# Head groups outside the batch rows, with the router, the shared slices and the expert tiles inside the attention steps

## The chip, the cores and the metric

One core of one Trainium2 chip runs the kernel. The metric is the device time of one execution in microseconds. The profile is of one execution. Names of engines: TensorE (PE in the rows, PEld its weight loads), VectorE (DVE), ScalarE (ACT), GpSimd (POOL) and SyncE (SP), which issues most of the DMAs.

## The reference, cut to what matters

```
x: [4, 512, 512]; xn = layernorm(x); out = x + attention(xn) + experts(xn)
attention, per batch row, 32 heads of 128 in 8 groups of 4 that share k and v, chunks of 128 tokens:
  q, k, v, gate = xn @ Wq.T, Wk.T, Wv.T, Wg.T;  rope on q and k
  dt = softplus(xn @ Win.T + dt_bias);  G = cumsum in the chunk of dt * -exp(A_log_bias)
  y = ((q k^T) * causal exp(G_i - G_j)) (v dt) + exp(G) q @ state;  state = exp(G_last) state + k_dec^T (v dt)
  y = y / rms(y) * gnorm_w * silu(gate);  sum over the heads of y @ Wo.T
experts, per token: 16 experts in 4 groups, best 2 groups by the router, best 2 experts in them;
  silu(x w1 + b1) * (x w2 + b2) @ w3 + b3, weighted, plus a shared one of 2 slices of 128
```

## The kernel before, in words

All products are made from high and low parts: each fp32 operand is copied to fp32r by ScalarE (the high part), the low part is the difference, made by POOL or VectorE, and `mm3` (L1083) issues three matmuls, high by high, high by low and low by high.

The kernel begins with a prologue that loads x, normalises 16 tiles of 128 tokens, turns them, computes the decay coefficients and the router's logits. The normalised and turned rows of the first half (two of the four batch rows) stay in SBUF as `xnh` and `xnl`; those of the second half go to memory. `end_phase` (L409) is where all engines meet before the first step.

Then `attention(half)` runs twice. In it a loop over the 8 head groups `kv` holds two steps, b = 0 and 1, one for each batch row of the half. So there are 32 steps in all, 16 in each half. `acc` holds the sums of 8 tiles in SBUF, and the weights of every head group are loaded and split in each half again. A step, on TensorE: projections of k, v and four heads of q, with transposes of v and k; the first out-projection (`out_proj`, L1125) of the step before, which lags one step; then the first gate projection, `scores(0)` (L1166), and a loop over the four chunks with the chunk's state (`chunk_state`), `inter`, a gate projection, `intra` (L1197), the next `scores`, `squares` and further out-projections. On VectorE: five ropes (`rope`, L1519), the low part of the values (`vw_lo`), of the fourth q (`q3lo`, L1582) and of k; then in the chunk loop `late_z` (L1497), `wlo`, `late_acc` (L1504), the state, its low part (L1621), `weigh` (L1543) and `gated` (L1565). ScalarE makes the high parts (`rope_hi`, `z_hi`, `vw_hi`, `split_hi` L811), the exponentials, the tanh of the gate (`silu_gate`, L921) and the rms batch (`rms_batch`, L858: two table loads, a Ln and an Exp over 2048 columns). POOL makes low parts (`split_lo` L643, `rope_lo`, `z_lo` L422) and the masked decay exponents (`gmasked`).

The order of each engine is written out by hand and kept by semaphores; an engine never passes over an instruction that waits. Weights come as pieces of 256 KB through two buffers, `stage`: SyncE issues piece n (`piece`, L439) when POOL has split piece n - 2, ScalarE then makes the high part and POOL the low part. `gload` (L489) brings the decay exponents of a chunk, broadcast to all partitions. On SyncE `hold` (L404) is a wait.

Between the halves stand the shared slices of the first half (`shared_up` L1288, `shared_down` L1308, `h_mul` L1654), the routing (`route_scores` L1682 to `route_slots` L1711) and the exchange of `acc` and xn. After the second half come the shared slices of that half and 48 expert tiles of 128 gathered tokens each: `turn_x` (L1340), `expert_up` (L1349), `turn_h` (L1362), `expert_down` (L1368). Their weights come in two DMAs per tile (`weights`, L583) into two buffers each; the expert's number is read from a table `etab` by SyncE. Last, the two picked rows of every token are gathered and added to the sums (`add_picked`, L1815).

```
e = sp.value_load(etab[0:1, bass.ds(k, 1)], min_val=0, max_val=E - 1)   # L584
hold(sp, m12_lo, k + 1)
sp.dma_start(raw12[par], row[:, 0:1024]).then_inc(m12_in[par], 16)      # L587
```

## Time and profile before

| | us |
|---|---|
| median of 3 runs (2355.04 to 2359.32) | 2358.24 |
| the profiled execution, its own time | 2350.6 |
| its span, first to last instruction | 2348.8 |

In the page of that execution TensorE is busy for 2134.9 us (91%), VectorE for 1836.9 (78%), ScalarE for 1403.2 (60%) and POOL for 1076.4 (46%), and 198.61 MB move by DMA. A row of a timeline gives the start, the duration, the engine, the line of the kernel, what is written and read, and in brackets the idle time ahead of it with what ended it. "issue" there means that the profile shows nothing that the engine waited for. A matmul's duration reaches from the start of its read to a modelled end, so successive ones overlap; the distance of the starts is its price. A window's row gives what each engine was busy in that stretch. TensorE's clock was granted in full (1.00, 2.4 GHz) or at half (1.2 GHz); the mean over the span is 0.973.

### The profile page before, as it was taken

The page shows a single profiled execution, that of the slowest core. Times are in us where ns is not written, and L with a number is a line of the kernel's source. Part 1 is how long each engine was busy: PE and PEld are TensorE (multiplying, and loading weights), DVE is VectorE, ACT ScalarE, POOL GpSimd, SP SyncE. Part 2 cuts the span into 40 slices and gives each one's busy share as a digit, 9 for nine tenths or more (in the row PEclk, how much of TensorE's full clock was granted, in tenths as well). Part 3 has the DMA queues.
Part 4 walks back from the last instruction along what each step waited for, and adds up shares of the span by engine and source line. Part 5 has one row for each costly group of instructions (what it writes and reads, how often), then busy time and mean ns, then how long its engine had stood idle before and what let it go on. Part 6 is the DMA issues. An engine that isn't in the chain of part 4 may idle for free.

```text
span 2348.8 us, 35057 instructions
## 1 busy us (share of the span) xinstructions
PE 2134.9 (91%) x9788; PEld 1687.2 (72%) x9788; DVE 1836.9 (78%) x3422; ACT 1403.2 (60%) x2716; POOL 1076.4 (46%) x840
## 2 busy tenths in 40 slices
PE   6599999999999999996999999999999999777884
PEld 6477777777777777774777777777777777555653
DVE  3488888888888888865888888888888888466665
ACT  2366666666666666653666666666666666455550
POOL 6245454545354544443454555454545455422216
PEclk9899999999999999997999999999999999898897
DMA  4312121212121212124121212121211121387777
GB/s 171 128 41 64 36 63 36 70 37 63 36 63 36 63 36 66 41 77 157 40 68 36 63 36 63 36 63 37 65 45 54 49 53 50 113 259 247 251 238 237
DMA packets 155566, 198.61 MB, mean 85 GB/s; under 512 B 13831, under 2 KB 90215, under 8 KB 155518
## 3 DMA queue, kind: packets, MB, share of 16 engines
q1 hardware_dynamic: 139742, 163.86, 23.8%
q0 software_dynamic: 7424, 21.00, 3.0%
q10 hardware_dynamic: 8352, 13.17, 1.5%
q8 instruction: 23, 0.38, 0.1%
q14 instruction: 25, 0.20, 0.0%
HBM read 169.65 MB, written 28.33 MB: 84 GB/s over the span
## 4 chain that ended last, share of the span: by engine, by line
issue 41%; POOL 26%; DVE 11%; PE 8%; DMA 7%; ACT 3%; SPq 2%; POOLq 1%; DVEq 0%; ACTq 0%
POOL gm L687 5%; POOL zl L425 5%; DMA gate<-in_wm 4%; POOL ql L694 3%; POOL wol L646 3%; POOL wgl L646 3%; POOL wql L646 2%; POOL vl L708 2%; DVE vwl L1557 1%; DMA gbc<-decay_exponents 1%; POOL kl L694 1%; DVE ql L1789 1%; POOL wkvl L646 1%; ACT qh L1030 1%; DVE yb L1501 1%
## 5 line engine op out<-in xcount | busy, mean ns | idle before, releaser
L425 POOL TENSOR_TENSOR zl<-yb,zh 128x512 fp32r<-128x512 f32 x130 | 172.6, 1328 | 348.5 <-ACT zh L872 348.3
L1085 PE MATMUL OU<-woh,zh 128*128 128x512 f32 x520 | 243.8, 469 | 16.3 <-POOL wol L646 11.9
L1085 PE MATMUL PJ<-xnh,wqh 128*128 128x512 f32 x544 | 225.9, 415 | 24.4 <-DVE t L1538 22.6
L1536 DVE TENSOR_TENSOR t<-PJ,cosb 128x512 f32<-128x512 f32 x160 | 110.2, 689 | 176.0 <-PE PJ L1087 132.8
L1087 PE MATMUL PJ<-xnh,wql 128*128 128x512 f32 x544 | 215.8, 397 | 0.0
L1086 PE MATMUL PJ<-xnl,wqh 128*128 128x512 f32 x544 | 215.3, 396 | 0.0
L890 ACT ACTIVATE qh<-t 128x512 fp32r<-128x512 f32 x128 | 81.0, 633 | 221.5 <-DVE t L1541 221.5
L1085 PE MATMUL PJ<-xnh,wgh 128*128 128x512 f32 x512 | 204.7, 400 | 0.0
L1087 PE MATMUL OU<-woh,zl 128*128 128x512 f32 x520 | 204.5, 393 | 0.0
L1086 PE MATMUL OU<-wol,zh 128*128 128x512 f32 x520 | 204.0, 392 | 0.0
L1087 PE MATMUL PJ<-xnh,wgl 128*128 128x512 f32 x512 | 200.4, 391 | 0.0
L1086 PE MATMUL PJ<-xnl,wgh 128*128 128x512 f32 x512 | 199.5, 390 | 0.0
L687 POOL TENSOR_TENSOR gm<-gbc,amask 128x512 f32<-128x512 f32 x128 | 166.1, 1298 | 49.6 <-DMA gbc<-decay_exponents 27.9
L1557 DVE SCALAR_TENSOR_TENSOR vwl<-vf,hcoef,vwh 128x128 fp32r<-128x128 f32 x384 | 180.3, 527 | 0.0
L646 POOL TENSOR_TENSOR wol<-stage,woh 128x512 fp32r<-128x512 f32 x64 | 88.7, 1406 | 169.7 <-ACT woh L814 169.7
L1541 DVE TENSOR_TENSOR t<-t 128x512 f32<-128x512 f32 x160 | 161.8, 1011 | 5.6
L897 ACT ACTIVATE gm<-gm,hcoef 128x128 f32<-128x128 f32 x512 | 162.1, 388 | 0.0
L646 POOL TENSOR_TENSOR wgl<-stage,wgh 128x512 fp32r<-128x512 f32 (+1 forms) x72 | 96.7, 1362 | 141.4 <-ACT wgh L814 141.4
L694 POOL TENSOR_TENSOR ql<-t,qh 128x512 fp32r<-128x512 f32 x96 | 137.1, 1440 | 41.4 <-ACT qh L890 41.4
L968 ACT ACTIVATE sth<-st 128x512 fp32r<-128x512 f32 x96 | 60.7, 633 | 144.6 <-DVE st L1612 96.5
L1085 PEld LDWEIGHTS PJ<-xnh,wqh 128*128 128x128 f32 x544 | 104.0, 191 | 58.7 <-DVE t L1538 38.4
L1085 PEld LDWEIGHTS OU<-woh,zh 128*128 128x128 f32 x520 | 98.1, 189 | 63.5 <-issue 41.3
(479 smaller groups left out, 6550.9 us busy)
## 6 DMA issues: line engine op xcount, KB each, us to landing
gbc<-decay_exponents SPq DMA_DIRECT2D x128, 256.0 KB, 4.8
gate<-in_wm SPq DMA_DIRECT2D x48, 512.0 KB, 4.5
stage<-in_wq SPq DMA_DIRECT2D x72, 256.0 KB, 3.9
stage<-in_wg SPq DMA_DIRECT2D x64, 256.0 KB, 2.7
stage<-in_wo SPq DMA_DIRECT2D x64, 256.0 KB, 2.7
gbc<-in_wm SPq DMA_DIRECT2D x48, 256.0 KB, 4.1
expert_rows<-rs ACTq DMA_DIRECT2D x48, 256.0 KB, 4.1
stage<-in_wkv SPq DMA_DIRECT2D x34, 256.0 KB, 2.7
```

The costliest lines, as they stand in the source:

```text
L425: nc.gpsimd.tensor_tensor(lo[:], yb[:, c, :], hi[:].bitcast(F32), ALU.subtract).then_inc(S["zlo"], 1)
L646: g.tensor_tensor(lo_out, stage[:, n[1], 0:lo_out.shape[-1]], hi_out.bitcast(F32), ALU.subtract).then_inc(wsplit_lo, 1)
L687: g.tensor_tensor(gm[:, c % 2, :].rearrange("p (h i) -> p h i", h=HG), gbc[:, c % 2, :].rearrange("p (h i) -> p h i", h=HG), amask[:].unsq ...
L694: g.tensor_tensor(lo, t2[:, (5 * b + i) % 2, :], hi.bitcast(F32), ALU.subtract).then_inc(S["ropelo"], 1)
L890: a.activation(hi, t2[:, (5 * b + i) % 2, :], ACT.Copy).then_inc(S["ropehi"], 1)
L897: ins = a.activation(gv, gv, ACT.Exp, bias=head(0, c, h))
L1085: nc.tensor.matmul(out_, a_hi, b_hi, start=first, stop=False)
L1086: nc.tensor.matmul(out_, a_hi, b_lo, start=False, stop=False)
L1087: return nc.tensor.matmul(out_, a_lo, b_hi, start=False, stop=last)
L1536: v.tensor_tensor(t1[:], PJ[bank][:], cosb[:], ALU.mult)
L1541: v.tensor_tensor(t2[:, slot, :], t1[:], t2[:, slot, :], ALU.add).then_inc(S["rope"], 1)
L1557: ins = v.scalar_tensor_tensor(vwl[:, hs], vf[:, c * P:(c + 1) * P], head(2, c, h), vwh[:, hs].bitcast(F32), ALU.mult, ALU.subtract)
```

## The change: what it does

The loop over head groups is outermost: for each of the 8 groups there are four steps, one for each batch row (b = 0 to 3), 32 in all, written out in full instead of two loops of eight turns. Each weight piece is loaded and split once. The turned rows of all four batch rows go to memory in the prologue and come back in every step (`xn_load`: eight loads of 256 KB into a ring of six). The sums of a batch row, `acc`, are 4 tiles; each is stored to memory after its add (`acc_store`) and loaded for another row (`acc_load`, which holds until the store has landed). The coefficients of a step are loaded too, sorted in memory; 16 copies on POOL sort them in the prologue.

The routing is cut into about 20 parts, each behind one rope of VectorE in steps 0 to 4. The scatters of the slot table stand on POOL in steps 5 to 10. In steps 4 to 11 (`SHARED`) TensorE does one batch row's part of a shared slice in chunk 3, and the down product is added to the next step's out-projections. In steps 13 to 28 each step carries three expert tiles u, u + 1 and u + 2 (`m` is true). The weights of a tile come in three pieces A, B and C through the same `stage` buffers; A and B are the up weights, C the down weights, and they share two pairs of SBUF tiles, so that B of tile v takes the place of C of v - 1. ScalarE makes the high and POOL the low parts (VectorE made the low parts before). The gathered rows, their parts and the bias rows have one buffer each. In steps 29 to 31 and at the end `late_acc` also adds the picked rows. At the end one flush of four out-projections remains. The bias of the down product comes as three small matmuls.

The core of the diff (SyncE, then ScalarE, TensorE and VectorE):

```diff
-HALVES = 2
-ROWS = B // HALVES
-NT = ROWS * NCH
-STEPS = KV * ROWS
...
+STEPS = KV * B
+SHARED = range(B, 3 * B)
+SCATTERED = range(5, 11)
+FIRST_EXPERT = 13
+LAST = STEPS - B
...
+    def unit_bias(v):
+        if v == 0:
+            At(sp, FIRST_EXPERT).before("oproj", 4)
+        else:
+            hold(sp, m_dn, v)
+        e = sp.value_load(etab[0:1, v:v + 1], min_val=0, max_val=E - 1)
+        row = bdram[bass.ds(e, 1), :, :].rearrange("o r n -> (o r) n")
+        sp.dma_start(plain(fhh[0:2, P:512]), row[:, 0:384]).then_inc(mb_in, 16)
+        sp.dma_start(plain(fhl[0:2, P:512]), row[:, 384:768]).then_inc(mb_in, 16)
...
+    def acc_store(s, c):
+        kv, b = (s - 1) // B, (s - 1) % B
+        At(sp, s).wait("accd", c + 1)
+        t = b * NCH + c
+        dst = out[t // NT, t % NT] if kv == KV - 1 else accd[t]
+        sp.dma_start(dst, acc[:, c, :]).then_inc(acc_out[c], 16)
+    def acc_load(s, c):
+        kv, b = (s - 1) // B, (s - 1) % B
+        hold(sp, acc_out[c], 16 * (s - 1))
+        t = b * NCH + c
+        sp.dma_start(acc[:, c, :], xv[:, t, :] if kv == 0 else accd[t]).then_inc(acc_in[c], 16)
...
-        with sp.Fori(0, KV) as kv:
-            for b in range(ROWS):
...
+        first_pieces((0, 1))
+        if m:
+            if u == 0:
+                unit_piece("A", 0)
+            unit_piece("B", u)
+            unit_bias(u)
+        gload(0)
+        gload(1)
+        if s >= 2:
+            acc_store(s - 1, 3)
+            acc_load(s, 3)
+        first_pieces((2, 3))
+        if s + 1 < STEPS:
+            hcoef_load(s + 1)
+            if s == 0:
+                hold(sp, x0_out, 32)
+                for j in range(4):
+                    hold(sp, xts_out[j], 96)
+            else:
+                At(sp, s - 1).wait("proj", 10)
+                if s - 1 in SHARED:
+                    hold(sp, u_up, s - B)
+            xn_load(s + 1, (0, 1))
+        gload(2)
+        if m:
+            unit_piece("C", u)
+            unit_piece("A", u + 1)
+        if m:
+            unit_bias(u + 1)
+            unit_piece("B", u + 1)
+            unit_piece("C", u + 1)
+            unit_piece("A", u + 2)
+        if s:
+            acc_store(s, 0)
+            acc_load(s + 1, 0)
+        if b == B - 1 and kv + 1 < KV:
+            for j in range(2):
+                piece(("wkv", kv + 1, j), wkv[kv + 1, j])
+        shared_piece(0)
+        shared_piece(1)
+        gload(3)
+        if m:
+            unit_bias(u + 2)
+            unit_piece("B", u + 2)
+        if s:
+            acc_store(s, 1)
+            acc_load(s + 1, 1)
+        if m:
+            unit_piece("C", u + 2)
+            unit_piece("A", u + 3)
+        if b == B - 1 and kv + 1 < KV:
+            piece(("wq", kv + 1, 0), wq[kv + 1, 0])
+            piece(("wq", kv + 1, 1), wq[kv + 1, 1])
+        if s:
+            acc_store(s, 2)
+        if b == B - 1 and kv + 1 < KV:
+            piece(("wq", kv + 1, 2), wq[kv + 1, 2])
+            piece(("wq", kv + 1, 3), wq[kv + 1, 3])
+        if s:
+            acc_load(s + 1, 2)
+        if s + 1 < STEPS:
+            at.wait("proj", 10)
+            if s in SHARED:
+                hold(sp, u_up, s - B + 1)
+            xn_load(s + 1, (2, 3))
+        shared_piece(2)
...
+        first_piece(1)
+        if m:
+            if u == 0:
+                split_hi(("A", 0))
+            split_hi(("B", u))
+        if s:
+            rms_batch(at)
+        if m:
+            x_hi(u, 0)
+        rope_hi(0, kh[:])
...
+        rope_hi(4, qh[:, 3, :])
+        if m:
+            h_hi(u)
+        if s:
+            z_hi(at, 1)
+        if m:
+            evict(u, 0)
+            x_hi(u + 1, 1)
+            split_hi(("B", u + 1))
+            store(u)
+        silu_gate(0)
+        if m:
+            m_tan(u + 1, 1)
+            split_hi(("C", u + 1))
...
+                at.wait("stt", c + 1)
+                if c:
+                    at.wait("yinter", c)
+                a.activation(sth[:], st[:], ACT.Copy).then_inc(S["sthi"], 1)
+                if m and c == 1:
+                    m_tan(u + 2, 2)
+                    split_hi(("C", u + 2))
+                    split_hi(("A", u + 3))
+                if b == B - 1:
+                    for j in (2 * c, 2 * c + 1):
+                        split_hi(("wkv", kv + 1, j) if j < 2 else ("wq", kv + 1, j - 2))
+                if b == 0 and s in SHARED and c == 0:
+                    split_hi(("ws", kv - 1, 0))
+                    split_hi(("ws", kv - 1, 1))
+                silu_gate(c + 1)
+                if m and c == 0:
+                    h_hi(u + 1)
+                    x_hi(u + 2, 2)
+                if m and c == 1:
+                    h_hi(u + 2)
+                exp_g(c + 1)
+            if c:
...
+        if m:
+            at.before("y", 4)
+            if u:
+                pe.wait_ge(m_h, u)
+            expert_up(u, 0)
+        for j in (2, 3):
+            at.wait("roperd", j)
+            proj_q(j)
+        if m:
+            turn_h(u)
+        if s:
+            if b == 1:
+                need(("wo", kv, 3))
+            out_proj(at, 0)
+        if m:
+            at.before("wsc", 4)
+            expert_down(u, 0)
+            turn_x(u + 1, 1)
+        if b == 0:
+            need(("wg", kv, 3))
+        at.wait("roperd", 4)
+        proj_g(0)
+        if m:
+            expert_up(u + 1, 1)
+        at.wait("ropelo", 4)
+        at.wait("q3lo", 1)
+        if m:
+            pe.wait_ge(m_ev, u + 1)
+        scores(0)
...
+            if m and c == 1:
+                expert_up(u + 2, 2)
+            if m and c == 3:
+                at.wait("stt", 3)
+                expert_down(u + 2, 2)
+            if s in SHARED and c == 3:
+                at.wait("stt", 3)
+                at.wait("gated", 3)
+                shared_up(s - B)
+            if s == RANKED and c == 3:
+                at.wait("stt", 3)
+                pe.wait_ge(rk_made, 1)
+                mflat = msum.rearrange("p t n -> p (t n)")
+                nc.tensor.matmul(CS[:, 0:256], upper[:], mflat, start=True, stop=True)
+                nc.tensor.matmul(CS[:, 256:512], ones[:], mflat, start=True, stop=True).then_inc(rk_done, 1)
+            if c < 3:
+                if c == 0:
+                    at.wait("roperd", 5)
+                else:
+                    at.wait("gated", c)
+                proj_g(c + 1)
+            if m and c == 0:
+                turn_h(u + 1)
+                turn_x(u + 2, 2)
+            if m and c == 1:
+                at.wait("yt", 1)
+                turn_h(u + 2)
+            intra(c)
+            if c < 3:
+                scores(c + 1)
+            if m and c == 0:
+                at.wait("stt", 1)
+                expert_down(u + 1, 1)
+            if c:
...
+        rope(0, 0)
+        if m:
+            x_low(u, 0)
+        rope(1, 0)
+        if s:
+            late_z(at, 0)
+        rope(2, 1)
+        if m:
+            h_of(u, 0)
+        rope(3, 0)
+        rope(4, 1)
+        if m:
+            h_low(u)
+        dve.wait_ge(hc_in[s % 2], 16 * (s // 2 + 1))
+        vw_lo(0)
+        at.wait("ropehi", 5)
+        v.tensor_tensor(ql[:, 3, :], t2[:, (5 * s + 4) % 2, :], qh[:, 3, :].bitcast(F32),
+                        ALU.subtract).then_inc(S["q3lo"], 1)
+        at.wait("knhi", 1)
+        v.tensor_tensor(knl[:], TR[:, 0:3 * P].rearrange("p (a b) -> p a b", a=3),
+                        knh[:].bitcast(F32), ALU.subtract).then_inc(S["knlo"], 1)
+        if s:
+            late_z(at, 1)
+        if m:
+            x_low(u + 1, 1)
+            gated(0)
+            h_of(u + 1, 1)
+        weigh(0)
...
+            if m and c == 0:
+                h_low(u + 1)
+                x_low(u + 2, 2)
+            if m and c == 1:
+                h_of(u + 2, 2)
+            at.wait("yintra", c + 1)
+            if c:
+                at.wait("yt", c)
+                v.tensor_tensor(yb[:, c, :], YI[:], yb[:, c, :], ALU.add).then_inc(S["y"], 1)
```

## Rows read from the trace of the kernel before

**Rows 1.** Windows by stage: length, busy us of each engine, PEclk, DMA share, GB/s
```profile
98.30:165.90 67.60, 54.13 (x242) 42.83 (x240) 48.81 (x90) 35.28 (x69) 24.42 (x18) 0.90 0.22 60
165.90:1015.10 849.20, 824.69 (x3783) 654.94 (x3781) 729.22 (x1366) 560.57 (x1098) 402.86 (x303) 1.00 0.19 51
1015.10:1071.90 56.80, 52.03 (x206) 38.57 (x204) 36.16 (x76) 19.15 (x26) 19.17 (x14) 0.97 0.36 105
1071.90:1154.30 82.40, 60.16 (x254) 47.75 (x253) 57.26 (x107) 37.61 (x73) 33.19 (x27) 0.83 0.30 96
...
2003.10:2042.00 38.90, 25.43 (x106) 19.87 (x105) 12.75 (x17) 18.57 (x24) 19.09 (x16) 0.87 0.33 106
2042.00:2285.00 243.00, 199.50 (x1040) 149.11 (x1040) 152.08 (x283) 141.77 (x280) 51.68 (x42) 0.91 0.78 247
```
**Rows 2.** Waits of TensorE over the span: us in total, times, longest
```profile
PE SC L1366 <- DVE gm L1804: 43.0, 36, 3.2
PE SC L1085 <- issue: 32.5, 32, 1.6
```
**Rows 3.** Timeline of one step, 392.35 to 448.90: start, us, engine, line, what
```profile
392.35 0.80 PE L1085 MATMUL PJ<-xnh,wkvh 128*128 128x512 f32 x1
...
411.30 0.47 PE L1085 MATMUL OU<-woh,zh 128*128 128x512 f32 x1 [0.74 <-POOL wol L646]
...
414.14 0.39 PE L1085 MATMUL PJ<-xnh,wgh 128*128 128x512 f32 x1
...
414.93 0.90 DVE L1541 TENSOR_TENSOR t<-t 128x512 f32<-128x512 f32 x1
...
416.80 0.68 DVE L1582 TENSOR_TENSOR ql<-t,qh 128x512 fp32r<-128x512 f32 x1
...
417.58 0.47 PE L1085 MATMUL SC<-qh,kh 128*128 128x512 f32 x1 [0.56 <-issue]
...
422.88 0.39 PE L1087 MATMUL SC<-qh,kl 128*128 128x512 f32 x1
...
424.75 0.62 ACT L814 ACTIVATE wkvh<-stage 128x512 fp32r<-128x512 f32 x1
...
424.87 0.69 DVE L1621 TENSOR_TENSOR stl<-st,sth 128x512 fp32r<-128x512 f32 x1 [0.70 <-ACT sth L968]
```
**Rows 4.** Timeline of TensorE over one expert tile
```profile
2185.60 0.59 PE L1085 MATMUL OU<-woh,vwh 128*128 128x512 f32 x1
...
2187.10 0.36 PE L1085 MATMUL TR<-qh,wkvh 128*128 128x256 f32 x1
...
2189.01 0.66 PE L1345 MATMUL PJ<-ident,vf 128*128 128x128 f32 x4
2189.42 0.48 PE L1085 MATMUL YE<-woh,vwh 128*128 128x512 f32 x1
```
**Rows 5.** Window of ScalarE's rms batch: length, busy us, PEclk, DMA share, GB/s
```profile
1021.73:1028.26 6.53, 6.49 (x4) 1.00 0.25 68
```
**Rows 6.** DMA issues by line: KB each, median us from issue to landing
```profile
stage<-in_wkv SPq DMA_DIRECT2D x16, 256.0 KB, 2.7
...
xnl<-turned SPq DMA_DIRECT2D x4, 256.0 KB, 5.1
...
out<-acc SPq DMA_DIRECT2D x8, 256.0 KB, 3.8
```
**Rows 7.** Timeline of SyncE's issues within one tile's loads
```profile
2101.96 0.29 SPq L592 DMA_DIRECT2D zh<-bias_rows  x1
...
2103.84 0.37 SPq L587 DMA_DIRECT2D gate<-in_wm  x1
```
**Rows 8.** POOL's low half of a weight piece, 150 to 1055: ns min/median/max
```profile
L646 POOL TENSOR_TENSOR wol<-stage,woh x32: 1271/1295/1762, 167.7 to 975.9; 128x512 fp32r<-128x512 f32 x32
```
**Rows 9.** Three windows of VectorE's router work between the halves, and their sum
```profile
sum 28.09, DVE 26.14; mean DVE 8.71
```
**Rows 10.** VectorE's add at the end of a rope: ns min/median/max
```profile
L1541 DVE TENSOR_TENSOR t<-t x160: 691/888/1779, 112.7 to 1969.2; 128x512 f32<-128x512 f32 x160
```

1934 lines of the change are left out of this document (861 added, 1073 removed).

## The prediction, made before the changed kernel was run

> **What bounds the kernel now.** The windows by stage come first [rows 1]. In the long attention stretch (15 steps in 849.2 us, so 56.6 us a step; the second half has the same) TensorE is busy for 97% of the time. The other time lies elsewhere: 98.3 us ahead of the first step, 67.6 us in that step, 56.8 us between the halves, 82.4 us in the first step of the second half, and 2348.8 - 2003.1 = 345.7 us at the end, 243 of it in the expert tiles. TensorE's own waits [rows 2] are few: inside attention mostly the one in front of the scores (32.5 us, 32 times), in the expert tiles 43 us on VectorE. Inside a step [rows 3] matmuls of 512 columns start every 0.227 us (13 of them, and the wait of 0.5, lie between 414.14 and 417.58). VectorE ends its low part of q (L1582, at 416.80 + 0.68) 0.1 us before the scores start at 417.58: the wait "issue" is a wait for VectorE. So TensorE sets the pace with VectorE just behind it, 48.6 us busy in the 56.6, and what is put into VectorE's row before the scores delays TensorE.
>
> **What the change removes.** The stage between the halves (56.8), the surplus of the second half's first step (82.4 - 56.6 = 25.8), and the whole end (345.7) go. Step 0 begins on TensorE at 98.3 but ends at 165.9; it now does no out-projection (48 matmuls x 0.227 = 10.9 us) and no rms batch. The exchange of phases stays: 16 small copies on POOL sort the coefficients where a memset of 1.8 us stood, about even. VectorE's 5.7 us of late work also go, so I let it end at 157, which is 8.9 less. Together 437.2; 2348.8 - 437.2 = 1911.6.
>
> **What comes back on TensorE.** Shared slices: 24 matmuls up and 12 down per step, 36 x 0.227 = 8.2, eight times = 65.4; the bias 16 x 0.227 = 3.6. An expert tile [rows 4]: up from 2187.10 to 2189.01 = 1.91, turning the rows to 2189.42 = 0.41, down and turning h 1.50 from 2185.60 to 2187.10, and 0.05 more since three small bias matmuls replace one: 3.87. Times 48 = 185.8. A tail now stands alone after step 31, which in the kernel before lies beside the shared slices: the sum of squares 1.2, table loads, Ln and Exp 6.5 (the whole of [rows 5]), z and its halves 2.9, four out-projections 10.9, the add 0.7, the store 3.8 to 4.3 [rows 6]: 26.6. So with every new wait at nothing: 1911.6 + 65.4 + 3.6 + 185.8 + 26.6 = 2193.0. That is the floor, 6.6% below now.
>
> **The waits that it adds.** One step with tiles (13 to 28) carries three. I walk it from its start, with durations from rows; "T" is the end of the first `expert_down`.
> 1. `h_low` of tile u stands behind the fifth rope on VectorE. In the step shown [rows 3] that rope ends 23.5 us after the start (414.93 + 0.90 against 392.35). `x_low` now waits for ScalarE's table work (+1.5) and `h_of` for its tanh (+1.7, of which 1.0 takes the place of a wait for ql): 25.7, then two ScalarE copies and `h_low`, 1.6: 27.3. TensorE ended its first out-projection at 21.8 (414.14), 0.74 of it waiting for wol; with `turn_x`, up and `turn_h` (2.4) and without that wait and a small one on ropes, it is there at 23.3. Wait 4.0.
> 2. Piece B of tile u+1. SyncE holds until T (`unit_bias` waits for `m_dn`), reads the tile's expert from the table (0.9), then does what lies between 2101.96 and 2103.84 in [rows 7]: two bias rows, a second reading, a hold, the issue. With 0.15 for its hold: T + 2.95. Landing 2.7 [rows 6], ScalarE's half 0.6, POOL's 1.3 [rows 8], hand-overs 0.25: T + 7.8. TensorE has only `turn_x` and one gate projection to do, 3.1. Wait 4.7. ScalarE stands in front of the same piece, and behind it wait the tanh of the gate, `gated` and the weighing of the scores.
> 3. `expert_down` of u+1 stands ahead of the out-projection and needs `h_low`, which stands behind the state's low part. In the step shown the scores end at 423.1 and that low part at 425.5 [rows 3]. With `h_low`: wait 2.6.
> 4. Piece B of u+2: again 7.8 from the second `expert_down`, against 2.7 + 0.7 + 1.4 = 4.8 of work. Wait 3.0, and the next `wfh` waits on ScalarE behind it.
> 5. `turn_h` of u+2 waits for that chain, 1.5.
> Sum 15.8; the wait before the scores and its neighbour, 1.5 to 1.6 a step now [rows 2], lie inside it: 14.3 net, x16 = 229. Bounds for this term: nothing, if SyncE and the queues run ahead of what I read; and 20 a step, if landings take the 3.8 to 5.1 us of the slower rows of [rows 6] and POOL's and ScalarE's queues slip as well.
>
> Smaller ones. **Router**: 26.1 us of VectorE, in three stretches now [rows 9], go into the ropes of steps 1 to 4, 6 to 8 a step. The idle time behind ropes 0 and 3 takes 3 of that: 17 remains. **xn loads**: in the shared steps four 256 KB loads are issued only when `shared_up` is done, 3.8 us before the step ends, and need about 6 (four issues, then 3.5 to 5.1 to landing [rows 6]): 2.2 x 8 = 18, and 2 elsewhere. In other steps they go out behind a store that must land; this just fits. **Steps with b = 3**: the pieces of wkv and wq stand on SyncE behind `acc_store`, and `acc_load` holds until that store has landed (3.8). ScalarE took the first at 424.75 in the step shown [rows 3], and would get it at 428.8; VectorE's 1.5 us of lead takes part. I take 5 us x 7 = 35 (between 0 and 10). The shared pieces likewise, 4 in all. **Picked rows**: two more VectorE adds per chunk (0.7 each) in steps 29 to 31: 13. The step's other loads and stores (2 MB of sums, 2 MB of xn) raise traffic from 51 to some 140 GB/s; the expert stage moves 247 [rows 1], so the bytes themselves cost nothing if the queue's order doesn't.
>
> Sum: 2193.0 + 229 + 17 + 20 + 35 + 4 + 13 = 2511 on the span of 2348.8. The profiled execution took 2350.6 and the median is 2358.2, 9.4 above the span: **2520**.
>
> **A rule against the change.** In this trace VectorE's add of two SBUF tiles (L1541) takes from 0.69 to 1.78 us, median 0.89 [rows 10], with the same operands each time, so what differs runs beside it. The change puts nine more POOL halves, 12 us, into each step with tiles. The Trainium skill, GPSIMD Engine Reference, Key points, says that GpSimd shares its SBUF interfaces with VectorE and contends with instructions that have two SBUF inputs. The median counted above leaves this out; it is the third rival.
>
> **Rivals.**
> A, faster: TensorE finds other work and the tiles cost what they do now, 243 / 48 = 5.06 us each, with the b = 3 terms gone: 2520 - 229 - 35 + 57 = **2313**. For it: the stage of now hides its weight loads with two buffers. Against it: one buffer of each kind, and SyncE's hold at T. It decides once the net wait in a tile step is under 4.2 us (14.3 - 162 / 16). Chance 0.25.
> B, SyncE's row: every `acc_load` waits for a landing, so gloads and xn are late in every step, 4 us x 31 less the 20 counted: **2625**. Against: a store lands in 3.8 [rows 6], and between two of them the step has 8 us or more; the loads are wanted a step later. Chance 0.12.
> C, VectorE beside POOL: of 12 us a quarter meets a two-input instruction (some 12 of its 48.6 us) and holds it up, 3 us x 16: **2568**. Chance 0.12.
> D, the unrolled steps feed TensorE too slowly. The unrolled tile stage shows 199.5 busy and 43 of named waits in its 243 us, so nothing is left for it. At 1 us a step: 2552. Chance 0.03.
>
> **The numbers.** My forecast has 0.48. A gives 0.22 faster and 0.03 within 0.2%, which is about what a measurement of this kernel can tell from no change; all others are slower: 0.24, 0.03, 0.73 with a little of the forecast's lower tail in the first. The forecast's own range is 2420 to 2615 (tile steps at 8 to 20 net); to hold 8 in 10 the whole reaches to 2300, which takes in A.
>
> **What would show it.** Steps without tiles at 57 to 59 us, shared ones at 67, tile steps at 80 to 85. In the list of TensorE's waits: the first matmul of `expert_up` on POOL's low half of a weight piece, 4 to 5 and 3 us, 16 times each; `expert_down` on VectorE's `mhl`. SyncE's holds on PE before the bias rows. A tail of 25 us. The forecast is wrong if tile steps stay under 72 us, or if steps without tiles are above 62.

## The result, and the profile after

The changed kernel takes 2656.1 us (median of 4 runs, 2650.8 to 2664.0) against 2356.9 of the kernel before in the same comparison: ratio 1.127, 95% interval 1.124 to 1.130. Slower, as forecast, but by 299 us where 162 were forecast, and 41 us above the upper end of the range. The profiled execution has a span of 2653.9 us, so 143 us more than the 2511 of the sum.

The windows by stage of the changed kernel, with the columns of [rows 1]: before step 0; step 0; steps 1 to 3; the shared steps 4 to 11; step 12; the 16 tile steps 13 to 28; steps 29 and 30; step 31 with the tail.

```profile
0.00:96.17 96.17, 58.80 (x265) 55.18 (x265) 38.73 (x74) 23.03 (x38) 43.17 (x38) 1.00 0.60 202
96.17:163.36 67.19, 50.16 (x204) 38.20 (x205) 45.34 (x86) 28.09 (x64) 20.77 (x29) 0.87 0.33 99
163.36:361.49 198.13, 179.79 (x775) 137.20 (x773) 169.28 (x320) 107.25 (x208) 64.23 (x49) 0.97 0.29 91
361.49:915.89 554.40, 517.63 (x2298) 403.93 (x2297) 431.39 (x751) 303.50 (x587) 227.23 (x178) 0.99 0.29 92
915.89:974.50 58.61, 57.67 (x264) 45.80 (x265) 51.35 (x93) 35.68 (x70) 24.60 (x18) 1.00 0.35 113
974.50:2433.06 1458.56, 1190.79 (x5186) 923.64 (x5185) 911.06 (x1633) 722.57 (x1448) 571.51 (x456) 0.91 0.36 112
2433.06:2564.07 131.01, 117.26 (x507) 89.46 (x505) 117.51 (x195) 69.76 (x136) 57.45 (x47) 0.96 0.39 117
2564.07:2653.90 89.83, 71.39 (x302) 56.02 (x300) 73.66 (x118) 43.48 (x75) 39.17 (x33) 0.91 0.31 94
```

Set against the sum, stretch by stretch: the end of step 0 is 6 us late (163.4 against 157), steps 1 to 12 take 811 us where 802 were summed, steps 29 to 31 with the tail 221 where it was 209. The tile steps take 1458.6, 91.2 each, where 83.9 were summed: 116 of the 143 us are there. TensorE is busy 82% of that stretch, 1190.8 us, and waits 267.8; its clock was granted at 0.91.

TensorE's waits over the span, for [rows 2]:

```profile
PE SC L1137 <- issue: 103.4, 31, 5.7
PE CS L1137 <- issue: 55.2, 16, 7.4
PE YE L1222 <- DVE upper L1673: 41.7, 23, 2.3
PE YI L1137 <- issue: 40.0, 17, 3.0
PE TR L1339 <- ACT vh L1031: 28.1, 10, 3.2
```

L1137 stands in the helper that issues the three products. The rows are mostly, in order, the waits ahead of `expert_down(u)`, `expert_down(u+1)`, `turn_h`, `expert_up(u+1)` and of K's transposes for V.

Three tile steps in a row, of batch rows 1, 2 and 3 (the same columns as above):

```profile
1339.21:1431.57 92.36, 74.49 (x326) 57.84 (x325) 58.24 (x103) 45.54 (x91) 36.39 (x29) 0.91 0.35 109
1431.57:1516.23 84.66, 71.45 (x326) 55.70 (x325) 56.01 (x103) 43.14 (x87) 31.23 (x25) 0.94 0.36 111
1516.23:1609.81 93.58, 75.52 (x327) 57.99 (x325) 55.98 (x103) 46.69 (x93) 38.89 (x31) 0.89 0.37 118
```

This pattern repeats through all 16: row 2 takes 84.7 to 86.0 us, rows 0 and 1 take 91.5 to 94.3, row 3 takes 93.2 to 95.0. All of them hold three tiles. TensorE's timeline in the middle one, only the instructions that it waited for:

```profile
1458.43 0.77 PE L1137 MATMUL SC<-fbh,fhh 128*128 128x512 f32 x1 [3.73 <-issue]
1468.37 0.36 PE L1137 MATMUL YI<-fah,fch 128*128 128x256 f32 x1 [2.83 <-issue]
1479.09 0.47 PE L1137 MATMUL CS<-fah,fhh 128*128 128x512 f32 x1 [2.46 <-issue]
1488.14 0.35 PE L1137 MATMUL TR<-fbh,fch 128*128 128x256 f32 x1 [1.11 <-issue]
1495.33 0.30 PE L1222 MATMUL YE<-ident,upper 128*128 128x128 f32 x1 [2.26 <-DVE upper L1673]
```

These are the five waits of the prediction, in its order: `expert_down(u)`, `expert_up(u+1)`, `expert_down(u+1)`, `expert_up(u+2)`, `turn_h(u+2)`. It had 4.0, 4.7, 2.6, 3.0 and 1.5, 15.8 in all; here they are 12.4. The waits were found, and in this kind of step they are shorter than forecast, so the surplus must come from elsewhere.

Step 17, of row 1, shows two sources. Its timeline on VectorE, GpSimd, ScalarE and TensorE:

```profile
1357.62 1.29 POOL L789 TENSOR_TENSOR ql<-t,qh 128x512 fp32r<-128x512 f32 x1
...
1358.87 1.29 POOL L467 TENSOR_TENSOR zl<-yb,zh 128x512 fp32r<-128x512 f32 x1
1359.46 3.76 DVE L1711 TENSOR_TENSOR t<-t 128x512 f32<-128x512 f32 x1
...
1360.12 2.55 POOL L711 TENSOR_TENSOR wol<-stage,woh 128x512 fp32r<-128x512 f32 x2
1363.25 0.63 ACT L982 ACTIVATE qh<-t 128x512 fp32r<-128x512 f32 x1 [2.58 <-DVE t L1711]
...
1373.49 0.77 PE L1137 MATMUL SC<-fah,fhh 128*128 128x512 f32 x1 [5.68 <-issue]
...
1377.21 0.63 PE L1138 MATMUL PJ<-xnl,wgh 128*128 128x512 f32 x1
1377.64 0.63 PE L1139 MATMUL PJ<-xnh,wgl 128*128 128x512 f32 x1
```

The addition of two SBUF tiles that ends a rope, 0.69 us at its shortest in [rows 10], takes 3.76 us. GpSimd works without a gap from 1357.62 to 1362.67, four operations of 1.3 us, and the addition ends 0.55 us behind the last. The 16 tile steps have eight such additions of 3.7 to 3.8 us, one in each step of rows 0 and 1, where the four pieces of wg or wo ("first pieces" below) are split. The kernel before never goes over 1.78. The last two rows show the second: after the wait of 5.68 us the products of 512 columns start 0.43 us apart, the lower level of the clock (1.2 GHz), not 0.23.

### The profile page after: what moved, and what is told of

Read it like the earlier page. It is cut to its first block, busy times and chain, and to the rows that moved or that the text cites. A ratio compares the mean times of both kernels' runs of the same rounds, so it can differ in the third digit from the quotient of the medians.

```text
span 2653.9 us, 32305 instructions
## 1 busy us (share of the span) xinstructions
PE 2243.5 (85%) x9788; PEld 1749.4 (66%) x9788; DVE 1838.3 (69%) x3263; ACT 1333.4 (50%) x2624; POOL 1048.1 (39%) x846
## 4 chain that ended last, share of the span: by engine, by line
PE 50%; DVE 15%; issue 13%; DMA 9%; ACT 7%; SPq 3%; POOL 2%; ACTq 0%; DVEq 0%; POOLq 0%
PE PJ L1137 7%; PE PJ L1139 7%; PE PJ L1138 7%; DMA stage<-in_wm 4%; PE TR L1310 3%; DVE vwl L1733 3%; PE OU L1137 3%; PE OU L1138 3%; PE OU L1139 3%; DVE t L1711 2%; PE YI L1137 2%; PE SC L1137 2%; PE YI L1138 2%; PE YI L1139 2%; DMA stage<-in_wq 1%
## 5 line engine op out<-in xcount | busy, mean ns | idle before, releaser
L1137 PE MATMUL OU<-woh,zh 128*128 128x512 f32 x500 | 250.4, 501 | 13.1 <-POOL zl L467 11.0
L1137 PE MATMUL PJ<-xnh,wqh 128*128 128x512 f32 x512 | 213.8, 418 | 17.9 <-DVE t L1708 17.6
L1137 PE MATMUL PJ<-xnh,wgh 128*128 128x512 f32 x512 | 222.0, 434 | 1.1 <-DVE t L1708 1.1
L1711 DVE TENSOR_TENSOR t<-t 128x512 f32<-128x512 f32 x160 | 209.9, 1312 | 5.5
L1138 PE MATMUL PJ<-xnl,wgh 128*128 128x512 f32 x512 | 212.5, 415 | 0.0
L1139 PE MATMUL PJ<-xnh,wql 128*128 128x512 f32 x512 | 203.9, 398 | 0.0
L1138 PE MATMUL PJ<-xnl,wqh 128*128 128x512 f32 x512 | 202.8, 396 | 0.0
L711 POOL TENSOR_TENSOR fal<-stage,fah 128x512 fp32r<-128x512 f32 x74 | 95.8, 1294 | 259.5 <-ACT fah L880 259.1
L711 POOL TENSOR_TENSOR fbl<-stage,fbh 128x512 fp32r<-128x512 f32 x74 | 95.2, 1287 | 235.5 <-ACT fbh L880 234.9
L1777 DVE TENSOR_TENSOR wfl<-gm,wfh 128x512 fp32r<-128x512 f32 x128 | 107.0, 836 | 115.5 <-ACT wfh L1071 114.3
L1310 PE MATMUL TR<-y,ones 128*128 128x512 f32 x256 | 138.9, 625 | 22.4 <-ACT y L1111 22.4
```

Of the source, the lines that this page charges most:

```text
L711: g.tensor_tensor(lo_out, stage[:, n % 2, :], plain(hi_out), ALU.subtract).then_inc(wsplit_lo, 1)
L1137: nc.tensor.matmul(out_, a_hi, b_hi, start=first, stop=False)
L1138: nc.tensor.matmul(out_, a_hi, b_lo, start=False, stop=False)
L1139: return nc.tensor.matmul(out_, a_lo, b_hi, start=False, stop=last)
L1310: nc.tensor.matmul(TR[:], ones[:], y2[:], start=True, stop=True).then_inc(S["ssq"], 1)
L1711: v.tensor_tensor(t2[:, slot, :], t1[:], t2[:, slot, :], ALU.add).then_inc(S["rope"], 1)
```

## The experiments

Unless said otherwise an experiment starts from the changed kernel. "Rows 0 and 1" are the steps of these batch rows, u to u+2 the three tiles of a step. A variant's line numbers are shifted by the lines that it adds. Each run has its own comparison with the kernel before, whose median there was 2353.2 to 2357.0.

**What the tiles cost.**

```
def has_units(s):
-    return FIRST_EXPERT <= s < FIRST_EXPERT + MT // 3
+    return False
```

> The expert tiles and the additions of the picked rows are left out; attention, router, shared slices and the round trips of the rows stay. Theory 1 (the tiles alone make the miss; the step with row round trips is worth what was predicted, 57 to 59 us): the 16 steps that held tiles fall from 91.2 to 58.5 us, 523 us in all, and with the picked rows gone the time is near 2125 us. Theory 2 (row round trips cost everywhere, hidden in the 91.2): these steps stay at 64 us or more, time 2210 us or more, and SyncE's row store is the wait ahead of TensorE. The granted clock of the stretch tells the rest: 0.91 with tiles; if it is 0.97 or more without them, the waits around the tiles pull the clock down.

The picked rows are neither gathered nor added. Measured 2108.9 us (one execution). Four of its steps, rows 1, 2, 3 and 0, as windows:

```profile
1209.88:1266.54 56.66, 55.33 (x255) 43.63 (x253) 48.60 (x91) 35.89 (x70) 22.73 (x17) 1.00 0.36 109
1266.54:1322.58 56.04, 54.96 (x255) 43.72 (x253) 50.05 (x91) 33.87 (x66) 16.90 (x13) 1.00 0.30 95
1322.58:1386.33 63.75, 57.50 (x255) 44.35 (x253) 51.43 (x91) 37.07 (x72) 24.42 (x19) 0.97 0.35 116
1386.33:1442.96 56.63, 55.06 (x254) 43.70 (x253) 48.51 (x91) 35.89 (x70) 22.75 (x17) 1.00 0.33 107
```

Theory 1. A step with its row round trips and xn loads costs what it cost before, 56.0 to 56.7, and 64 to 66 in row 3. So the prediction's rival B is dead, and so is anything else that would make all steps long, unrolled code among it. The granted clock of the 16 steps is 0.99, where it was 0.91 with tiles. Here the first pieces cost 0.6 us: rows 0 and 1 are nearly as short as row 2. Only together with tiles do they cost 7 us. Row 3 is 8.7 us longer than row 2 on average here, and 8.6 with tiles: its surplus is not of the tiles. Row 2 with tiles (84.66) less row 2 without (56.04) less the tiles' own 11.6 leaves 17.0. Of this 12.1 are waits (13.2 against 1.1), the last 0.8 of them at the squares, and 4.9 are TensorE's own time. Nearly all of the 4.9 is the lower clock: the same step of e18_spread (at the end), at 1.00, has 67.1 us of own time where this one has 71.4.

**The load of piece B** (waits 2 and 4), the same exchange for u + 2.

```
-                    unit_bias(u + 1)
                     unit_piece("B", u + 1)
+                    unit_bias(u + 1)
```

> Piece B of tiles u+1 and u+2 is issued ahead of the hold for the bias row, not behind it. Theory 1 (the load of piece B behind expert_down is what the up-projections wait for, my waits 2 and 4): the YI wait of 1.4 to 2.8 us and the TR wait of 1.3 us go in each of 16 tile steps, 54 us in all, time near 2602 us. Theory 2 (ScalarE and GpSimd, whose splits of B stand behind the row transposes and the expert_down of the tile before, are the late ones): no more than 10 us, time 2646 to 2656 us. Theory 3 (waits also cost clock): over 54 us, time below 2595 us, granted clock of the tile stretch up from 0.91 to 0.93.

Measured 2581.3, ratio 1.096 (1.095 to 1.098), 75 us less. SyncE's issues around one tile in this kernel:

```profile
1376.72 0.35 SPq L478 DMA_DIRECT2D stage<-in_wm  x1
1378.02 0.31 SPq L494 DMA_DIRECT2D fhh<-bias_rows  x1
1378.52 0.25 SPq L495 DMA_DIRECT2D fhl<-bias_rows  x1
```

The piece is now ahead of the bias rows; in the changed kernel it left 1.8 us behind the first of them (1461.69 and 1463.50). In a row 2 step the waits of 2.83 and 1.11 are gone and the step is 81.8 us long, 2.8 shorter; rows 0 and 1 gain 4.5 on average and row 3 5.2. The granted clock of the tile stretch did not rise (0.90, from 0.91), so theory 3's reason fails though its number holds. TensorE's waits in the 16 steps fell from 268 to 204 us, more than the 54 counted; what else stood behind this piece was not parted further.

**Where the first pieces cost.** First their order on SyncE and ScalarE, then their absence, then half of their low parts alone.

```
 unit_piece("B", u) ahead of first_pieces((0, 1)); on ScalarE:
-    first_piece(0); first_piece(1); split_hi(("B", u)); rms_batch(at)
+    split_hi(("B", u)); rms_batch(at); first_piece(0); first_piece(1)
```

> In all steps with tiles piece B of tile u is loaded and split ahead of the two first pieces of wg or wo, and ScalarE splits these two behind the batch of the root mean squares, not ahead of it. Theory 1 (in the steps of batch rows 0 and 1 ScalarE's 4 us wait for piece B holds back the root mean squares, the late z and V's split): these 8 steps lose about 7 us each, 56 us, time near 2600 us, and the 3.0 us wait of the k transposes for V is gone. Theory 2 (only that 3.0 us wait was on the path): 24 us, time near 2632 us. Theory 3 (the lateness is absorbed by the wait ahead of expert_down that follows): under 8 us, 2648 to 2656 us.

2660.1, ratio 1.130: nothing, theory 3's number. Step 17 shows that its reason is another. The first row is VectorE's, the second, in its own fence, TensorE's:

```profile
1358.79 5.81 DVE L1712 TENSOR_TENSOR t<-t 128x512 f32<-128x512 f32 x1
```

```profile
1366.12 0.48 PE L1223 MATMUL YE<-ident,upper 128*128 128x128 f32 x1 [4.05 <-DVE upper L1674]
```

The wait for V ahead of K's transposes (3.04 us) is gone, and the one ahead of `expert_down(u)` fell from 5.68 to 3.17, so it absorbed nothing. But the addition that took 3.76 us takes 5.8 now, in all eight steps of rows 0 and 1: four GpSimd operations of 1.3 us end before it does, not three. And `turn_h(u)` waits 4.05 us where it waited 0.65. What the new order gave at the start of the step was lost at VectorE's addition.

```
-        first = [(("wg", "wo")[b], kv, j) for j in range(4)] if b < 2 else []
+        first = [(("wg", "wo")[b], kv, j) for j in range(4)] if b < 2 and not m else []
```

> From the changed kernel, the steps with tiles neither load nor split new pieces of wg and wo: the output projection and the gate keep the weights of the group before, so the output is not the reference's. Theory 1 (the first pieces, by the splits on ScalarE and GpSimd and the additions of the rope that VectorE can't finish while GpSimd works without a gap, make the steps of rows 0 and 1 7 us longer than those of row 2): these 8 steps fall to 85 to 86 us, 56 us in all, time near 2600 us, and no rope addition takes over 2 us (14 do now, the longest 5.0). Theory 2 (row 2's steps are short for another reason): 8 us or less, 2648 us or more.

2592.4 us (one execution), 64 less, theory 1: rows 0 and 1 fall to 83.8 to 86.4 us, rows 2 and 3 stay.

```
 def split_lo(name):           (GpSimd; third and fourth piece, tile steps)
-    g.tensor_tensor(lo_out, stage[:, n % 2, :], plain(hi_out), ALU.subtract)
+    g.tensor_tensor(lo_out[:, 0:8], stage[:, n % 2, 0:8], plain(hi_out)[:, 0:8], ALU.subtract)
```

> From the changed kernel, in tile steps GpSimd leaves out the low parts of the third and fourth first piece but for 8 columns (the gate and the output projection then use old low parts); all else stays, ScalarE's splits and all loads too. Theory 1 (GpSimd's work without a gap stops VectorE's additions of two SBUF operands, and that makes most of the first pieces' 8 us a step): the seven additions of 3.8 us in tile steps fall under 2, steps of rows 0 and 1 fall by 2 to 4 us, 16 to 32 us in all, time 2624 to 2640 us. Theory 2 (ScalarE's wait for piece B at the start, and the lateness that follows from it, make it all): within 6 us, 2650 to 2662 us.

2621.0, ratio 1.114 (1.111 to 1.117), 35 us less, just past theory 1's range. The only thing removed is 1.7 us of GpSimd in each of 8 steps (the two halves take 0.85 us, not 2.55), and GpSimd is idle 60% of the time. In the tile steps no such addition takes 3.7 us any more, and step 17 falls from 92.4 to:

```profile
1331.13:1418.32 87.19, 75.15 (x326) 58.34 (x325) 54.86 (x103) 45.50 (x91) 35.29 (x29) 0.90 0.37 116
```

So 35 of the 64 us come by GpSimd's work on the third and fourth first piece. In step 17 the addition ends 21.4 us after the start of the step, not 24.0, and the wait ahead of `expert_down(u)` falls from 5.68 to 2.09. How much of the 35 us comes by VectorE's addition, and how much since GpSimd's own later halves are earlier, no run parts; nor were the other 29 parted further.

**The clock.**

```
 at.before("wsc", 4)
+filler(SC, 12)
 expert_down(u, 0)
...
+filler(CS, 8)
 expert_down(u + 1, 1)
```

> From the changed kernel, TensorE does 12 products of 128x512 that nobody reads ahead of the wait for tile u's hidden part and 8 ahead of that for tile u+1's, 4.6 us at full clock into waits of 3.4 to 5.7 and 2.5 to 7.4 us. Theory 1 (the clock falls in the waits, and a step pays for it behind them: 74.4 us busy against 68.3 priced at full clock): granted clock of the tile stretch up from 0.91, the time falls by 20 to 60 us, to 2596 to 2636 us, though work was added. Theory 2 (the granted clock is a matter of heat or of the mean load, not of these waits): the clock stays or falls and the time stays within 10 us or rises by up to 16 x 1 us.

2648.2, ratio 1.126 (1.124 to 1.129). The tile stretch:

```profile
974.50:2424.15 1449.65, 1243.83 (x5507) 971.86 (x5505) 908.42 (x1633) 721.82 (x1448) 572.26 (x456) 0.93 0.36 113
```

The clock rose from 0.91 to 0.93 as theory 1 has it, the time fell by 8 us, which the intervals don't tell from nothing. TensorE's timeline says why:

```profile
1466.05 0.55 PE L1137 MATMUL YI<-fah,fch 128*128 128x256 f32 x1 [4.00 <-issue]
```

This is `expert_up(u+1)` in row 2: its wait is 4.0 us, against 2.83 without the fillers. The products ahead of it took 2.3 us less, and half of that was waited for again, since piece B sets the time there. Behind the longer wait the clock fell, where it had stayed whole: products of 256 columns start 0.21 us apart, not 0.12. TensorE's own time in this step, less the 20 fillers at 0.23 us, is 71.2 us, as in the changed kernel (71.4). So here the fillers moved the lower clock and didn't remove it; what the whole of it costs, this run doesn't tell.

**Moving instructions in their engines' order.** The fences of this part name the moves in short; most of their lines are not code. Each kernel builds on the one named in its expectation. Four moves together:

```
 early B(u+1), B(u+2); B(u) ahead of the first pieces, as above; and
-    rope_hi(4, ...); h_hi(u)         DVE: rope(4, 1); h_low(u)
+    h_hi(u); rope_hi(4, ...)         DVE: h_low(u); rope(4, 1)
 row 3: wkv pieces issued ahead of acc_store(s, 0), split behind exp_g
```

> Four moves at once: piece B of u+1 and u+2 ahead of the bias hold; piece B of u ahead of the first pieces and these behind the root mean squares; in batch row 3 the next wkv pieces issued ahead of the row's store and split behind h of tile u+1; tile u's h evicted and its low part taken ahead of the last query rope. Theory 1 (the waits are independent and each move takes its own): 54 + 56 + 4 x 4.8 + 16 x 4.0 = 193 us, time near 2463 us. Theory 2 (behind each wait removed stands another chain nearly as late, at the vector engines): half of it, near 2560 us. Theory 3 (TensorE's clock rises as the waits go, 0.91 to 0.95 in the tile stretch): 230 us or more, time below 2430 us.

2537.5, ratio 1.077 (1.074 to 1.079): 119 us less, between theories 1 and 2. Wait 1 is gone, and wait 2 has come back with 4.2 us: ScalarE has z(1), the high part of the gated rows, in front of evicting tile u and of piece B. The addition of 5.8 us of e2_b_first is here too. The next kernel moves those:

```
 ScalarE: split_hi(B, u+1); x_hi(u+1); evict(u); store(u); z_hi(1)
 ScalarE: h_hi(u+1) ahead of sth of chunk 0; m_tan(u+2) ahead of sth of chunk 1
 VectorE: x_low(u+1) ahead of knl; h_low(u+1), h_of(u+2) ahead of the state
 SyncE:   C(u+2), A(u+3) ahead of acc_store(s, 1)
```

> The four moves of e6_four and these: ScalarE splits piece B of tile u+1 and takes its rows ahead of evicting tile u and of z(1), GpSimd and VectorE in the same order; tile u+1's h is evicted and its low part taken ahead of the state's, tile u+2's tanh and h ahead of the state of chunk 1; SyncE issues C(u+2) and A(u+3) ahead of row store 1. Theory 1 (the waits that were left, 4.2 us ahead of expert_up(u+1), 1.5 to 2.5 ahead of expert_down(u+1), 2.2 ahead of turn_h(u+2), are only the place of these instructions in their engines' order, and each is followed by half clock): 16 x (4.2 + 1.5 + 2.0 + 2.2) = 158 us below e6_four, time near 2380 us, tile steps of row 2 near 71 us. Theory 2 (the attention's own chain is made late instead, above all by h ahead of the state): half, near 2460 us. Theory 3 (GpSimd is the bound in tile steps): no more than 40 us, 2497 us or more.

2454.0, ratio 1.043 (1.041 to 1.045), 83 us less, theory 2's number. Rows 1, 2 and 3:

```profile
1285.20:1365.85 80.65, 70.95 (x327) 54.82 (x325) 61.15 (x103) 45.19 (x91) 37.03 (x29) 0.96 0.41 126
1365.85:1440.40 74.55, 67.71 (x326) 52.65 (x325) 55.96 (x103) 43.02 (x87) 31.51 (x25) 1.00 0.41 125
1440.40:1516.90 76.50, 69.16 (x326) 53.79 (x325) 55.45 (x103) 45.90 (x93) 39.18 (x31) 0.98 0.46 145
```

The clock of this row 2 step is whole again, with no filler: waits of 2.3 us and less didn't lower it there. In the other three steps of row 2 it was 0.98.

```
 on GpSimd and ScalarE: pieces 1, 2 behind vl / vh, pieces 3, 4 behind rope_lo(2)
```

> e9_order, and in tile steps the first two pieces of wg or wo are split behind V, and GpSimd takes the other two behind the low part of the second query rope, so that it waits for VectorE's addition ahead of them. Theory 1 (VectorE's additions from SBUF wait until GpSimd makes a gap; one of them takes 5.8 us in e6_four, and 4.0 us ahead of turn_h(u) come of it): 8 steps x 4 = 32 us below e9_order and no rope addition over 3 us. Theory 2 (the pieces are then themselves late at out_proj(0) or proj_g(0)): the time rises by 8 x 1 to 3 us.

2471.8, 18 us more than e9_order: theory 2. The additions are short (none over 1.8 us in the tile steps), but now TensorE waits 2.7 us for wo at `out_proj(0)` in row 1 and 5.9 to 6.1 for tile u's h in row 0.

```
 VectorE: st of chunk 0 copied ahead of late_acc and vw_lo
 SyncE:   B(u+2) ahead of acc_store(s, 0), but for row 3
 all:     the next group's four wg pieces at the end of row 3's step
```

> e9_order, and: the next group's wg pieces are loaded and split at the end of the step before (GpSimd stands idle there for 15 us); VectorE copies the state of chunk 0 ahead of the row sum and V's low part; piece B of tile u+2 is issued ahead of row store 0 and the load of the decay exponents. Theory 1 (each of these is again only a matter of place: 2.4 us ahead of expert_up(u+2), 1.5 ahead of expert_down(u+1), 5 to 6 us of the steps of row 0): 16 x 2.3 + 16 x 1.5 + 7 x 5 = 96 us below e9_order, time near 2358 us, steps of rows 0 and 2 alike at 71 us. Theory 2 (the end of row 3's steps has no room for four more splits): rows 0 gain 5 and rows 3 lose 5, time near 2393 us. Theory 3 (SyncE's earlier hold for piece B delays the row's load): 2410 us or more.

2413.2, ratio 1.024 (1.023 to 1.026). Row 2 is at 69.8 us and row 0 at 70.7 to 72.3, but row 3 at 81.4 to 83.0. The pattern is theory 2's; the number lies 20 us above it, where theory 3 has it. The squares of row 3 wait for ScalarE, which stands in front of the third wg piece:

```profile
1515.93 2.07 PE L1331 MATMUL TR<-y,ones 128*128 128x512 f32 x2 [7.87 <-ACT y L1132]
```

> e11_more, and in the tile steps of batch row 1 GpSimd takes the low parts of the third and fourth wo piece behind that of the second query rope, and the low part of the third query rope ahead of pieces C(u) and A(u+1), so that it waits for VectorE twice in a stretch it now works through without a gap. Theory 1 (VectorE's addition of two SBUF operands waits for a gap of GpSimd: 5.8 us where it takes 0.7 alone): the 4 us wait ahead of turn_h(u) in row 1 falls to 1 or less, 4 x 3 us, time 12 us below e11_more. Theory 2 (the pieces are late instead, as in e10_gap): equal or up to 10 us slower.

2430.0, 17 us more than e11_more. Moving two low parts on GpSimd behind rope 2 took the 4.05 us wait of row 1 down to 1.6 and brought 2.7 at wo and 3.5 at `expert_down(u)`: theory 2, worse than its bound. A gap for VectorE made on GpSimd is paid for on GpSimd.

```
+def first_of(s): wg or wo pieces 2, 3   (start of the step)
+def last_of(s):  wg or wo pieces 0, 1   (end of the step before)
```

> e9_order with the two moves of e11_more that are not about wg (state ahead of the row sum; piece B of tile u+2 issued early), and in place of its third: of each group's wg and wo only the first two pieces are loaded and split at the end of the step before, the other two at the start of the step; in steps without tiles the pieces stay ahead of the root mean squares. Theory 1 (in e11_more a step of row 3 pays 7.9 us because ScalarE waits for pieces 3 and 4 with y's square behind them, and a step of row 1 pays 4 us because GpSimd works without a gap on four wo pieces): rows 3 fall from 82 to 75 us, rows 1 from 76 to 72, rows 0 rise by 1 to 2; 7 x 7 + 6 x 4 - 7 x 2 = 59 us below e11_more, time near 2354 us, that of the kernel before. Theory 2 (the two pieces at the start still stop VectorE): rows 1 stay at 76, time near 2378 us. Theory 3 (the clock or SyncE bounds row 3): 2400 us or more.

2382.9, ratio 1.011 (1.009 to 1.014), theory 2's number: row 3 fell to 75 us, but rows 0 and 1 are at 74 to 77, with an addition of 3.3 to 3.4 us in each of them from step 16 on.

```
 VectorE, start of the step, rows 0 and 1: the low parts of the two first pieces
 ScalarE: pieces of last_of(s) ahead of the third sum of squares; evict(u+2) behind y's square
```

> e13_halves, and: in tile steps VectorE takes the low parts of the two first pieces itself at the start of the step, where it stands idle for 2.7 us, and ScalarE splits them ahead of the root mean squares; the two pieces at the end of a step are split ahead of the third sum of squares, and tile u+2 is evicted behind y's square. Theory 1 (VectorE's additions of two SBUF operands wait for gaps of GpSimd: 3.4 us for one of them in each step of rows 0 and 1 of e13_halves, 2 us of it passed on to turn_h(u)): no such addition over 2 us in the tile steps; rows 0 and 1 fall from 75 to 72 to 73 us, all steps lose 0.4 to 0.8 us ahead of the last squares; 8 x 2.5 + 16 x 0.5 = 28 us below e13_halves, time near 2355 us, equal to the kernel before. Theory 2 (the first rope of the step, late by the two low parts, holds TensorE's second projection instead): within 8 us of e13_halves, 2375 to 2391 us.

2352.4, ratio 0.999 (0.998 to 1.000), theory 1's number, and level with the kernel before. No addition in the tile steps is over 2 us, and a low part costs VectorE 0.7 us where it cost GpSimd 1.3. But the number is partly luck. The profiled execution is 37 us shorter than that of e13_halves. Rows 0 and 1 of the tile steps give 11 of these (1.4 us a step), the whole tile stretch 14, and steps 0 to 12, where VectorE takes no low part of a piece, 15. One wait was new, at the first query projection of rows 0 and 1; moved, it turned into another of the same size:

> e14_dve, with VectorE's two low parts behind the first rope and the copy of V, where it stands idle for 2 us, not ahead of them. Theory 1 (the 2.8 us wait of TensorE's first query projection for the first rope in rows 0 and 1 is the place of these two): the wait goes, 7 steps x 2.8 = 20 us, time near 2332 us. Theory 2 (they then hold the low part of tile u's rows, and expert_up(u) waits instead): within 6 us of e14_dve, 2346 to 2358 us.

2351.4, ratio 0.999: theory 2 in number, though it is not `expert_up(u)` that waits but K's transposes, for V. The first row is of e14_dve, the second, in its own fence, of e15_slot, both TensorE's timeline in row 1:

```profile
1261.31 0.51 PE L1170 MATMUL PJ<-xnh,wqh 128*128 128x512 f32 x1 [2.76 <-DVE t L1741]
```

```profile
1272.22 0.52 PE L1372 MATMUL TR<-ident,t 128*128 128x128 f32 x3 [2.58 <-ACT vh L1058]
```

> e15_slot, and in the steps without tiles from step 5 on (5, 8, 9, 12, 29) the two first pieces are split by ScalarE behind V, not ahead of the root mean squares, and their low parts are VectorE's, behind the second rope. Theory 1 (these pieces make V late in these steps: the transposes of K wait 2.7 us for it in step 5): 3 steps x 2.7 + 2 x 1 = 10 us below e15_slot. Theory 2 (V's wait only moves to the scores, for which the third rope is then late): within 3 us of e15_slot.

2356.8, ratio 1.001: no gain, rather 5 us lost, more than theory 2's 3. In step 5 the wait for V went, and one of 2.8 us at the third query projection came. The steps ahead of the tiles stay where they were, and their share of the miss is not explained further.

```
 ScalarE: first_piece(0) ahead of the root mean squares, first_piece(1) behind V
 VectorE: low part 0 behind rope 0, low part 1 ahead of h_of(u)
```

> e15_slot, with only one of the two first pieces split ahead of the root mean squares; the other behind V, its low part on VectorE ahead of tile u's h, where it waits for ScalarE anyway. Theory 1 (the 2.6 to 2.9 us wait of K's transposes for V in rows 0 and 1 is ScalarE's chain piece B, two first pieces, root mean squares, rows of the tile, K, V; row 2, without the two pieces, has no wait): the wait falls under 1 us, steps of rows 0 and 1 from 73.5 to 71.5 us, 7 x 2 = 14 us, time near 2337 us, below the kernel before by over its spread. Theory 2 (the wait goes on to expert_down(u) through VectorE's later ropes): within 5 us of e15_slot, 2346 to 2357 us.

2330.9 (2328.3 to 2333.9), ratio 0.990 (0.988 to 0.992): theory 1. It is 325 us below the changed kernel and 1% below the kernel before, with the change's own structure, its traffic and all its matmuls. The tile stretch, then steps 17 to 20:

```profile
959.81:2108.01 1148.20, 1082.92 (x5187) 848.28 (x5185) 884.25 (x1650) 716.90 (x1448) 568.24 (x441) 0.99 0.46 142
1250.06:1320.31 70.25, 67.03 (x326) 52.71 (x325) 55.83 (x106) 44.04 (x89) 32.28 (x25) 1.00 0.46 141
1320.31:1389.15 68.84, 67.08 (x326) 52.74 (x325) 54.25 (x103) 43.00 (x87) 32.14 (x25) 1.00 0.43 135
1389.15:1464.13 74.98, 68.29 (x327) 52.70 (x325) 56.92 (x103) 47.77 (x96) 42.04 (x33) 1.00 0.49 151
1464.13:1534.80 70.67, 66.82 (x325) 52.68 (x325) 54.34 (x104) 44.54 (x90) 35.11 (x27) 1.00 0.48 146
```

Row 2 at 68.8 us is within 1.2 of 56.04 + 11.6, the step without tiles and the tiles' own work. The tile stretch is 310 us shorter than in the changed kernel, with the same products: 202 of these are waits (65 left of 268), 108 are TensorE's own time (1082.9, from 1190.8), with the clock granted at 0.99 and not 0.91. The lower clock went with the waits.

## Why the prediction was right, and where it failed

**Right.** What bounds: TensorE, with 56.6 us a step; e5_no_tiles has 56.0 to 56.7. The price of a tile on TensorE, 3.87, three times 11.6: row 2 of e18_spread confirms it within 1.2 us. The five waits, their places and order, and for row 2 their sum, 15.8 against 12.4; rows 0 and 1 have a sixth, of some 3 us, of K's transposes for V. Bytes showed no cost: traffic rose from 51 to 112 GB/s in the changed kernel, and to 142 in e18_spread, which is faster. Row 3's surplus, 5 taken with bounds of 0 and 10: 8.7 without tiles, 8.6 with. Tile steps at 80 to 85 held for row 2 alone, within 1 us. Steps without tiles were to take 57 to 59: step 12 has 58.6, but steps 2 and 3 (65.5 and 71.1, with router parts) and 29 and 30 (66.8 and 64.2, with picked rows) are over the 62 that was named as a sign of being wrong.

**Wrong, and by how much.** The tile stretch took 116 us more than was summed. The sum can be set against it in two ways.

By what TensorE did. The sum has 16 x 66.7 = 1067 us of its own time (56.6 less 1.5 of waits, and 11.6) and 275 of waits (15.8 in every step, 20 for row 3 and 2 for xn). The stretch has 1190.8 and 267.8. So the waits in all were sized right, and the step that failed is "matmuls of 512 columns start every 0.227 us", carried over to steps with 17 us of waits in each. The lower clock was a term put at nothing, without a reason, though it had been visible ahead, at 0.91 in the expert stage of [rows 1]. It measured 124 us, 7.7 a step, or 108 against the own time that e18_spread has for the same products. This is its share of the time and not what a full clock alone would give back: no run takes the lower clock away and leaves the waits, and where e8_fill tried it at two places a step it won 8 us at most.

By the kind of step:
- 58 us, 8 steps x 7.3, are the first pieces in rows 0 and 1: 5.1 of waits a step, 2.1 of TensorE's own time. The step that failed is "One step with tiles (13 to 28) carries three. I walk it from its start": it took all 16 for alike. It counted GpSimd's nine halves for the tiles and not that in half of the steps four more already stand in the same queue. e7_no_first gives 64 for them, e16_no_low gives 35 to GpSimd's part. Rival C named that mechanism, by the addition of two SBUF operands, and at 48 us its size was near; it was wrong in two things. It spread the cost over all 16 steps, and it added it as a rival of 0.12 where the traces bore both it and the forecast. The Trainium skill, SBUF — State Buffer, SBUF: two separate sides, has the shared port pair as an exclusive lock, which whoever starts first holds for the whole instruction. By that rule one instruction of 1.3 us is waited for; the trace has an addition waiting for three in a row.
- 44 us, 16 x 2.8, are what every step has, as row 2 shows it: 85.4 on average where 82.6 were summed (56.6, 11.6, the "14.3 net" and the share of xn). Its waits are 2.8 us shorter than the 15.8 forecast, and its own time is 5.7 us longer, the lower clock.
- 14 us, 4 steps x 3.6, are row 3, 8.6 where 5 was taken.

The remaining 27 us (step 0, the shared and router steps, the end) are each under 12, and no run here parted them.

**The rivals.** A was that tile steps could be had with almost no wait. It was wrong for this kernel and right about the structure: e18_spread is there, with 2331 for its 2313. Its "against", one buffer of each kind and SyncE's hold at T, named a matter of order as if it were one of structure: e1_b_early undoes the hold by exchanging two lines. B fell with e5_no_tiles. So did D: its unrolled steps take 56.0 to 56.7 us.

**The range** ended at 2615 since 20 us net was the upper bound of what a tile step adds beside its work. With row 3's surplus of 8.6 taken out, the 16 steps come to 20.8 (91.2 - 56.6 - 11.6, less 8.6 / 4), just over that bound, and the 27 us elsewhere come on top. The range had room for longer waits and none for the clock.

## What to carry to other kernels

When work from a stage of its own is woven into steps that already carry something, walk every kind of step, not one, and for each engine write down the longest stretch it would work without a gap; a half-idle GpSimd in front of additions of two SBUF tiles is not free. An added wait is often a matter of place: list what stands between the instruction and its release on each in-order queue, move it, and expect the next chain to be nearly as late, since here twelve kernels of moves led to 325 us, and several of them gave nothing. A lower granted clock is first a sign of waits, and it goes with them: when steps are to get many new waits, price their products between the two levels that the rows show, and don't expect fillers alone to win it back.
